# A fused attention and mixture-of-experts layer: moving the projection's transfers, asking later for landings, and adding the second expert's rows in the transfer

## The reference, cut to what matters

```python
xn = _layernorm(x)                       # x: (4, 1024, 256) float32, 4096 tokens
x + attention(xn) + experts(xn)
# attention: 16 heads of 16, causal, with a bias by distance; ctx @ Wo + bo
# experts: 8 experts, every token goes to 2 of them, weighted
logits = rms_scaled(xn) @ router_logits
_, choices = approx_max_k(logits, k=2)
gate_out = ragged_dot(sorted_xs, w_gate, group_sizes)
activation = gelu(gate_out[:, 0]) * gate_out[:, 1]
expert_outputs = ragged_dot(activation, linear, group_sizes)
out = einsum('blkd,blk->bld', unsorted(expert_outputs), combine_weights)
```

## Time and profile before

| | |
|---|---|
| median of three runs | 814.10 us (813.83 to 814.95) |
| the profiled execution | 815.55 us, span 813.8 us |
| DMA traffic | 98.20 MB, 74,912 packets |
| projection, attention, experts, combine | about 0 to 120, 120 to 549, 549 to 781, 781 to 814 us |

### The profile page before, as it was taken

The page is one execution under the profiler, slowest core; times in us unless marked ns, Lnnn a source line. Parts: engine busy times, 40 slices in busy tenths (PEclk is TensorE's granted clock), DMA queues, the critical chain, the costliest instruction groups (busy, mean ns, idle before and its releaser), DMA issues.

```text
span 813.8 us, 17685 instructions
## 1 busy us (share of the span) xinstructions
PE 766.9 (94%) x6172; PEld 468.4 (58%) x6172; DVE 546.2 (67%) x1419; ACT 466.9 (57%) x984; POOL 433.7 (53%) x561
## 2 busy tenths in 40 slices
PE   8999999999999999999999999879899899998997
PEld 6555554444444434444444444328889789888976
DVE  5458879999999888888888888303344334433348
ACT  3564567777777677777777777774333333333310
POOL 7665542231324545655475453264686667666676
PEclk9999999999999999999999999999999999999999
DMA  8895562513233134243442350113533333322777
GB/s 202 250 296 175 171 190 57 157 34 91 81 93 99 40 96 131 61 103 106 107 98 66 95 158 16 36 41 88 155 104 111 111 105 111 104 84 83 235 247 240
DMA packets 74912, 98.20 MB, mean 121 GB/s; under 512 B 16588, under 2 KB 54092, under 8 KB 74764
## 3 DMA queue, kind: packets, MB, share of 16 engines
q1 hardware_dynamic: 65960, 78.34, 34.2%
q0 software_dynamic: 8864, 18.72, 7.4%
HBM read 63.53 MB, written 30.75 MB: 116 GB/s over the span
## 4 chain that ended last, share of the span: by engine, by line
PE 50%; POOL 13%; issue 12%; ACT 4%; DVE 3%; DMA 2%; another core or an unknown queue 1%; DVEq 0%; POOLq 0%; ACTq 0%
PE banks L1154 17%; PE banks L754 16%; PE banks L746 13%; POOL expert_rows L1243 7%; POOL stacks L593 5%; ACT probs L1092 4%; PE banks L1339 3%; DVE stacks L1438 2%; PE banks L1348 1%; DMA stacks<-xn_rows,places 1%; DVE junk L708 1%; PE banks L1269 0%; DMA w_gu<-expert_rows 0%; DMA expert_rows<-stacks,places 0%
## 5 line engine op out<-in xcount | busy, mean ns | idle before, releaser
L708 DVE CUSTOM_DVE_ANT_0 junk<-banks,mask 128x128 bf16<-128x128 f32 (+7 forms) x512 | 359.6, 753 | 55.7 <-issue 50.6
L1092 ACT ACTIVATE probs<-banks 128x512 f32<-128x512 f32 x576 | 310.7, 606 | 102.7 <-PE banks L754 98.4
L754 PE MATMUL banks<-stacks 105*128 105x512 bf16 (+3 forms) x768 | 199.4, 329 | 10.1 <-issue 5.4
L746 PE MATMUL banks<-stacks 102*128 102x512 bf16 (+3 forms) x768 | 172.6, 326 | 2.2 <-DVE maxima L708 2.0
L885 POOL TENSOR_SCALAR_AFFINE_SELECT probs<-probs 128x512 f32<-128x512 f32 x128 | 79.9, 643 | 103.3 <-ACT probs L1092 99.5
L1321 DVE TENSOR_TENSOR probs<-banks,probs 128x256 f32<-128x256 f32 x71 | 30.1, 423 | 150.6 <-ACT probs L1285 125.0
L754 PEld LDWEIGHTS banks<-stacks 105*128 105x128 bf16 x768 | 65.6, 97 | 103.5 <-ACT probs L1092 40.5
L1154 PE MATMUL banks<-probs,ctxT 128*17 128x256 f32 (+2 forms) x1920 | 114.4, 360 | 2.0 <-DVE banks L1073 1.1
L1243 POOL DMA_INDIRECT expert_rows<-stacks,places x71 | 79.9, 1126 | 62.4 <-ACT stacks L1290 48.1
L746 PEld LDWEIGHTS banks<-stacks 102*128 102x128 bf16 x768 | 69.1, 98 | 72.2 <-DVE maxima L708 17.5
L1285 ACT ACTIVATE probs<-banks 128x256 f32<-128x256 f32 x71 | 27.3, 385 | 109.7 <-PE banks L1339 66.4
(11 more groups left out here) (129 smaller groups left out, 781.2 us busy)
## 6 DMA issues: line engine op xcount, KB each, us to landing
stacks<-qk_parts SPq DMA_DIRECT2D x192, 128.0 KB, 3.1
qk_parts<-ctxT SPq DMA_DIRECT2D x32, 384.0 KB, 3.3
xn_rows<-probs SPq DMA_DIRECT2D x8, 512.0 KB, 5.1
ctxT<-inverse_sums SPq DMA_DIRECT2D x8, 512.0 KB
w_gu<-in_w_gu SPq DMA_DIRECT2D x8, 512.0 KB
stacks<-in_x SPq DMA_DIRECT2D x16, 256.0 KB
ctxT<-expert_rows SPq DMA_DIRECT2D x16, 256.0 KB, 3.6
w_gu<-expert_rows SPq DMA_DIRECT2D x16, 256.0 KB, 5.5
```

Source lines behind the costliest of these rows:

```text
L708: last = dve.tensor_tensor_reduce(junk[:, n % RING, c:c + w], mpsum[:, slot, c:c + w], keep["mask"][:, S - w:S], 1.0, 3 * NEG, ALU.add, AL ...
L746: last = pe.matmul(mpsum[:, slot, at + c:at + e], qs[hq][0:R_MAX, h, qt * P:(qt + 1) * P], ks[hq][0:R_MAX, h, c:e], start=True, stop=True)
L754: last = pe.matmul(score_bank(("S", n, h))[:, c:c + w], ks[hq][:, h, kt * P:(kt + 1) * P], qs[hq][:, h, q0:q0 + w], start=True, stop=True)
L1092: act.activation(probs[:, u % PRING, h], score_bank(("S", n, h)), ACT.Exp, scale=SCALE).then_inc(exp_done, 1)
```

## The change

Three groups of edits:

- Projection. SP issues the input prefetch of a chunk after that chunk's four stores and no longer between them; the map, the scales and the eight constants go behind the stores of chunk 0. DVE normalises chunk 1 one quarter earlier, before the second split of chunk 0 and no longer before the third. PE takes the early product of place 7 after value tile 3 instead of 2.
- Experts. Up to tile 47 POOL asks for the landing of the scatter seven tiles back, not three; at tile 48 it catches up with five calls, and then goes on as before.
- Combine. SP no longer loads the k = 1 rows. POOL, instead of its 16 adds, issues 16 transfers that read the k = 1 rows and add them to the buffers holding the k = 0 rows. DVE adds the sum to `acc` in one step.

```diff
+SOON_FROM = 48
         def stores(c, par, load):
             sp.wait_ge(xn_ready, c + 1)
             sp.dma_start(xn_rows[ds(c, 1)].rearrange("a p t d -> (a p) t d"), xn[:, par]).then_inc(x_stored[par], 16)
-            if load:
-                sp.dma_start(x_in[:, c % XR], x_rows[c + XR]).then_inc(x_loaded[c % XR], 16)
...
                 if (c, q) in ROWS_AT:
                     load_rows(sp, scratch, heads, 0, *ROWS_AT[c, q])
-
-        sp.wait_ge(unused_set, 3)
-        (map, escale, 4 x (c_q, c_k))
+            if load:
+                sp.dma_start(x_in[:, c % XR], x_rows[c + XR]).then_inc(x_loaded[c % XR], 16)
+
         for c in range(NC):
             stores(c, c % 2, c + XR < NC)
+            if c == 0:
+                sp.wait_ge(unused_set, 3)
+                (map, escale, 4 x (c_q, c_k))
...
-                if (c, q) == (0, 2):
+                if (c, q) == (0, 1):
                     normalise(1, 1, 0)
...
-                if nxt and t in (0, 2):
-                    early(c, 6 + t // 2)
+                if nxt and t in (0, 3):
+                    early(c, 6 + t // 3)
...
         for s in range(NST):
-            if s >= LANDING:
-                landed(s - LANDING)
+            for done_s in [s - RR + 1] if s < SOON_FROM else range(s - RR + 1, s - LANDING + 1) if s == SOON_FROM else [s - LANDING]:
+                if done_s >= 0:
+                    landed(done_s)
             scatter(s)
...
-        sp.wait_ge(before["y_free"], RR + NST)
-        sp.wait_ge(before["w_ready"], NST)
-        for n in range(NP):
-            load(1, n)
...
     def on_gpsimd(pool):
-        pool.wait_ge(before["bias_set"], NP)
         for n in range(NP):
             pool.wait_ge(loaded[0][n], 16)
-            pool.tensor_tensor(flat(acc[:, 2 * n:2 * n + 2, :]), flat(acc[:, 2 * n:2 * n + 2, :]), flat(yk[0][n]), ALU.add).then_inc(first_ready, 1)
+            pool.dma_start(yk[n], y_rows[1][:, 2 * n:2 * n + 2, :], accum_op=ALU.add).then_inc(loaded[1][n], 16)
...
     def on_vector(dve):
+        dve.wait_ge(before["bias_set"], NP)
         for n in range(NP):
             rows = acc[:, 2 * n:2 * n + 2, :]
-            dve.wait_ge(first_ready, n + 1)
             dve.wait_ge(loaded[1][n], 16)
-            dve.tensor_tensor(flat(rows), flat(rows), flat(yk[1][n]), ALU.add).then_inc(second_ready, 1)
+            dve.tensor_tensor(flat(rows), flat(rows), flat(yk[n]), ALU.add).then_inc(second_ready, 1)
```

More of the change, by code:

```diff
@@ L345, in stores @@
                     load_rows(sp, scratch, heads, 0, *ROWS_AT[c, q])
-        sp.wait_ge(unused_set, 3)
-        sp.dma_start(scratch["map"].rearrange("(p s) c -> p (s c)", p=P), unused[:, :, :].rearrange("p s c -> p (s c)")).then_inc(map_stored, 16)
-        sp.dma_start(keep["escale"][:, :], ins["expert_scale"].partition_broadcast(P)).then_inc(map_stored, 16)
-        for q in range(NQ):
-            sp.dma_start(heads["qs"][q][R_ALIBI:R_MAX, :, :], ins["c_q"][q]).then_inc(heads["const_in"], 16)
-            sp.dma_start(heads["ks"][q][R_ALIBI:ROWS, :, :], ins["c_k"]).then_inc(heads["const_in"], 16)
+            if load:
+                sp.dma_start(x_in[:, c % XR], x_rows[c + XR]).then_inc(x_loaded[c % XR], 16)
         for c in range(NC):
             stores(c, c % 2, c + XR < NC)
+            if c == 0:
+                sp.wait_ge(unused_set, 3)
+                sp.dma_start(scratch["map"].rearrange("(p s) c -> p (s c)", p=P), unused[:, :, :].rearrange("p s c -> p (s c)")).then_inc(map_stored, 16)
+                sp.dma_start(keep["escale"][:, :], ins["expert_scale"].partition_broadcast(P)).then_inc(map_stored, 16)
+                for q in range(NQ):
+                    sp.dma_start(heads["qs"][q][R_ALIBI:R_MAX, :, :], ins["c_q"][q]).then_inc(heads["const_in"], 16)
+                    sp.dma_start(heads["ks"][q][R_ALIBI:ROWS, :, :], ins["c_k"]).then_inc(heads["const_in"], 16)
     def on_gpsimd(pool):
@@ L1375, in combine @@
     w_o, w_in, acc = last_weights["w_o"], last_weights["in"], last_weights["x"]
-    done_w = Room(keep["w_gu"][:, :, :].rearrange("p e h -> p (e h)"))
     halves = [Room(keep["ctxT"][:, 2 * m + 1]) for m in range(NP // 2)]
-    yk = [[halves[n // 2]([P, 2, D]) for n in range(NP)], [done_w([P, 2, D]) for _ in range(NP)]]
+    yk = [halves[n // 2]([P, 2, D]) for n in range(NP)]
     proj = keep["banks"][:, 0:PROJ]
@@ L1381, in combine @@
     out_done = sem("out_done")
-    proj_ready, first_ready, second_ready, pair_done = (sem(name) for name in ("proj_ready", "first_ready", "second_ready", "pair_done"))
+    proj_ready, second_ready, pair_done = (sem(name) for name in ("proj_ready", "second_ready", "pair_done"))
     flat = lambda a: a.rearrange("p t d -> p (t d)")
@@ L1387, in on_sync, with load @@
     def on_sync(sp):
-        def load(k, n):
-            sp.dma_start(yk[k][n], y_rows[k][:, 2 * n:2 * n + 2, :]).then_inc(loaded[k][n], 16)
+        def load(n):
+            sp.dma_start(yk[n], y_rows[0][:, 2 * n:2 * n + 2, :]).then_inc(loaded[0][n], 16)
         sp.wait_ge(before["scaled"], NP)
@@ L1397, in on_sync @@
                 sp.wait_ge(loaded[0][n - IN_FLIGHT], 16)
-            load(0, n)
-        sp.wait_ge(before["y_free"], RR + NST)
-        sp.wait_ge(before["w_ready"], NST)
-        for n in range(NP):
-            load(1, n)
+            load(n)
         for n in range(NP):
```

## The result

The change made the kernel slower: 823.28 us (median of four runs, 821.63 to 825.57) against 814.53 us (four runs of the kernel before beside them), a ratio of 1.0111, 95% interval 1.0073 to 1.0149, so +9.0 us (5.9 to 12.1). The prediction was 809.2 us, 807.0 to 816.0. The profiled execution took 821.85 us, its span is 820.0 us, 6.2 more than before.

What follows compares the result with a forecast made beforehand. PE was taken to bound the projection and nearly fill the experts, DVE to pace the combine. Gains of 2.7 (projection), 0 (experts) and 2.2 us (combine) gave 814.1 - 4.9 = 809.2 us, range 807.0 to 816.0.

Steps and rivals of the forecast that it cites:

- The combine's movement term: Combine: adding 256 KB by transfer takes 0.69 to 1.38 us a pair, taken as 0.9.
- the projection's 2.7 us: Projection: net gain from 1.8 + 0.7 + 0.9 - 0.7, bounds 0.3 and 3.6 us, kept through the attention.
- The store's term: Combine: storing a pair's result takes DMA 0.69 us, making 1.59 us a pair with the adding transfer.
- The first sum: Combine: the first pair's sum is there at about 785.5 us, where DVE could begin at 784.40 before.
- PE becomes the bound at 1.75: Combine: PE at 1.75 us a pair outlasts DVE 1.33, POOL 1.5 and DMA 1.59; gain 2.3, taken as 2.2.
- the first rival: Combine: transfers read twice, DMA bounds at 2.07 us a pair; loss 3.7 us, middle 1.4, total 812.8; chance 0.27.
- the 1.8 taken: Projection, chunk 1: with the queue empty at 17.5 us, 1.8 of the 1.93 us lost there is regained.
- the 0.7 taken: Projection, chunk 0: normalising a quarter earlier regains 0.7 of 0.93 us; lower bound a loss of 0.8.
- the 0.9 taken: Projection, place 7: PE does value tile 3 during DVE's maximum, so about 0.9 of 1.21 us goes.
- the cost of the moved constants: Projection: stores behind the ten moved transfers land 1 to 2 us later; chunk 3 waits up to 1.5, taken 0.7.
- the sign that I named for it: Projection: an ACT DMA wait near 36 to 50 us would show the 0.7 us cost was too small.
- The third rival: Projection: constants delay stores of chunks 1 and 2, so the 2.7 us gain does not arrive; total 812.2; chance 0.11.

Runs made afterwards that it cites:

- e5: Kernel before with the changed combine, but POOL's 16 transfers overwrite the buffers and add nothing: 820.81 us against 823.4 for before, ratio 0.9981.
- e6: Kernel before with the changed combine, but SP stores no result until all sums have landed: 833.95 us (two runs), ratio 1.0118 to before.
- e9: Kernel before with only the map, scales and constants moved behind chunk 0's stores: 789.31 us against 786.33 for before, ratio 1.0034.
- e7: e4 plus eight loads of the constants' sizes, spread over 128 partitions, behind chunk 0's stores: 820.06 us, ratio 0.9958 to before.
- e8: Kernel before with the projection's edits except the move of map, scales and constants, which stay ahead of the first store: 821.01 us, ratio 0.9973.
- e4: Kernel before with the projection's edits, but map, scales and constants right behind chunk 0's row store, ahead of its quarter stores: 812.85 us, ratio 0.9977.
- e3: Kernel before with only the later landings up to tile 48 in the experts: 814.73 us, ratio 0.9998 to before.
- e10: Kernel before, but DVE adds the lower expert's rows of pairs 0 to 5, POOL the other ten, no adding transfer: 784.09 us, ratio 0.9977.
- e1: Kernel before with the changed combine alone, all else untouched: 821.80 us, ratio 1.0094 to before.
- e12: e10 plus the projection edits of e4 (constants behind the first row store), against the kernel before: 781.12 us, ratio 0.9931.
- e11: e10 plus the projection edits of e8 (constants ahead of the first store), against the kernel before: 780.45 us, ratio 0.9931.

## Why the prediction was wrong

**The combine's movement term was mis-sized, and that was enough to turn the sign:** with the projection's 2.7 us gained as forecast, the combine's 7.5 would still have made the kernel slower. The terms around it held: DVE's adds take 0.69, POOL issues in 1.24 (predicted 1.2), and PE's 96 matmuls take 20.99 us when nothing delays them (e5). The step "256 KB moves in 0.69 to 1.38 us, I take 0.9" failed: it is 1.37 alone (e6), the upper bound, and with the store 2.20 instead of 1.59 a pair. The store's term, 0.69, was a little small too: 0.77 alone (e6). The first sum was forecast 1.1 us later than before; it came 2.4 later, and e5, where nothing is added, has the 1.1 (its first sum is 6.4 us behind the last scatter, against 5.3 before and 7.7 after). The step after it, "PE becomes the bound at 1.75", falls with it. It was the first rival, with its mechanism word for word: DMA share full to the end, DVE waiting for each landing, pairs over 1.75 us apart. The rival's price was 3.7 us where the combine lost 7.5. Of the missing 3.8, 2.1 are sixteen times the 0.13 by which a pair of the full stretch (2.20) is over the rival's 2.07; 0.08 of the 0.13 is the store's own price. The other 1.7 I put, as an estimate, at the two ends, where the rival had the engines full and they were not: their share was 0.40 from 780 to 785 us, since the first transfer landed 4.6 us after POOL's issue, against 2.8 after SP's, and 0.73 from 815 on, when the last sum still had two adds and a store before it. And I had shrunk the rival to a middle of 1.4 us, by the guess that reading a buffer on the core might be cheap; no row supported that.

The choice between the bounds was the error of method. I had written that the value is taken by the row it is nearest to, and there was none; 0.9 was taken because it kept DMA under PE's 1.75. The rule from the Trainium skill (Collectives: The Full Stack, section on why ReduceScatter is half of AllGather: an add in the path doubles the source reads on the same ring) gave 1.38. The trace agrees: 192 GB/s (e6) against 381. It deserved the larger chance.

**The projection: the gains came, the cost was over six times too small.** Chunk 1 went from 13.52 to 11.59 (1.93 against the 1.8 taken). That 1.93 was the loss in one trace; in the six of before it goes from 1.2 to 6.6 us (after e9). Chunk 0's idle time is gone, 0.93 against the 0.7 taken: from its transposes to chunk 1's it is 9.11 us, against 10.04. Place 7 waits 0.31 us instead of 1.21, the 0.9 taken:

```profile
64.55 0.61 PE L748 MATMUL banks<-stacks 102*128 102x512 bf16 x3 [0.31 <-DVE maxima L710]
```

The failed step is the cost of the moved constants, taken at 0.7 with an upper case of 1.5. It was 4.7 us in chunk 2, so the stretch to the attention lost 2.3 (1.7 from chunk 0's transposes on) where it was to gain 2.7. The place was right (chunk 3 waits for stores of chunk 1) and so was the sign that I named for it, a wait near 36 to 50 us. The size failed for two reasons. I set the slow stretch of the narrow transfers against the idle share of the DMA engines from 30 to 40 us, as if the narrow ones took their time out of that idle share and delayed nothing else. The engines were then busy 0.87 from 28 to 36 us, not full, and the stores behind the constants still landed 9.4 us after their issue; equal bytes over 128 partitions cost nothing (e7). And I had no term for PE's clock, 1.8 of the 4.7. The third rival, the gain not arriving, had the mechanism and stopped at zero gain where it was a loss of 2.3. Ahead of the first store or in the gap behind it (e8, e4) the transfers cost at most 1 us in chunk 1: no quarter store follows them for 4 us or more.

A rule of the Trainium skill bears on the narrow transfers (DMA: Bandwidth & Descriptors, sections on why a DMA increments its semaphore by 16 and on the rules for kernel authors): a transfer whose outermost size is 6 or 9 is spread over at most that many of the 16 engines. No view here shows the engines one by one, so the trace does not test it; e7's result is in line with it, and so it would be if the long rows were the cause.

**Experts.** Nothing, as predicted (e3: 0.9998).

Both losses are of one kind: work was put where a landing is what the next engine waits for.

## What to carry to other kernels

Adding in a transfer saves an engine's add and cost the DMA engines here as much as a second plain transfer; it pays only where they have that much room, and here the stretch was already at a share of 1.09. Where only bounds are known and one of them is the value that a mechanism gives, price the edit at that end. Put small narrow transfers where nothing that is awaited stands behind them, and look for idle time on an engine that can already do the add (7.4 us of DVE here; the gain in e10 is not clear of none by itself) before handing the work to the transfers.

## What the runs showed of the hardware

- An adding transfer into the core's buffers moves 192 GB/s (e6) where plain loads and stores together move 381 and stores alone 339 (e6), and costs POOL 1.24 us to issue instead of 0.72 (e5), for 256 rows of 1 KB. The plain issue is below the 0.98 us of a scatter of 128 rows; my lower bound was above it.
- A PE that idled 2.80 us was then granted 0.50 of its clock from 42 to 44 us, with 0.87 and 0.78 in the 2 us on either side, and that cost another 1.8 us. In e1, with the projection of before, the same happened in chunk 1: 2.40 us idle, then eight matmuls in 5.40 us, so that the chunk took 16.47 us where the trace of before has 13.52. Its PE had idled there too (1.77 us) and kept its clock. Of the nine traces with a stall in the projection, the three with 1.04 to 1.77 us of idle time kept it and the six with 2.40 and more lost it; in the combine, 2.4 us of idle time were followed by the lower clock in e10 and e12 and not in e11, and 3.0 us in e1 and not in the changed kernel. So undoing such a wait can give back more than the wait.

```profile
28.76 5.40 PE L564 MATMUL banks<-probs,ctxT 128*128 128x512 f32 x8 [2.40 <-DVE ctxT L484]
34.00 1.04 PE L541 MATMUL banks<-ident,probs 128*128 128x128 f32 x8
```

- A scatter that POOL issues beside DVE's adds takes longer. In e10 the last two scatters took 1.27 and 1.50 us beside DVE's six adds; before they take 0.97 each. In e11 and e12 they took the same 1.50. That is up to 0.8 us of what the shared adds gain. POOL's plain loads in e5 were not slowed: 746 to 789 ns, with DVE adding from the fifth on. A sentence of the Trainium skill fits both (SBUF — State Buffer, section SBUF: two separate sides): DVE with two inputs from the buffers takes the port that it shares with POOL only against a POOL operation that reads the buffers, and the scatter has its list of places there. No run here varied what POOL reads.

```profile
745.12 1.27 POOL L1243 DMA_INDIRECT expert_rows<-stacks,places  x1 [1.68 <-ACT stacks L1290]
746.69 1.50 POOL L1243 DMA_INDIRECT expert_rows<-stacks,places  x1 [0.30 <-issue]
```

- The three chips differ by 4.7% for the same kernel. The projection takes the same time where it is that of before and keeps its clock (first product of the attention at 123.47 in the trace of before, 123.11 in e5 on the second chip, 123.48 in e10 on the third). The attention takes 423 to 427 us in e1 to e4, 428 to 432 in e5 to e8 and 412 to 414 in e9 to e12; from its end to the last scatter it is 229 to 232, 230 to 233 and 209 to 213. The single instructions of the attention take the same on them (from 130 to 500 us DVE's maxima 753 ns in before, 752 in e8 and 753 in e10, PE's score products of L754 329, 329 and 328); it is the idle time between them that is less: 7.2 us in before, 10.5 in e8 and 1.4 in e10 ahead of those products, most of it put down to nothing that the profile shows. Why is open.
